# A two-stage image network on one core: fewer rows in the copies of offsets, and residuals kept in the padded image

## What is computed

```python
x = x + _L0_conv_ref(_gn(x), L0_conv_sigma)        # gaussian blur, 11 x 11
x = x + _L1_conv_ref(_gn(x), ...)                  # 3 x 3 conv -> one gate per image and channel; silu(x*scale + 0.1*x)
x = x + _L2_conv_ref(_gn(x), ...)                  # snake convolution: 9 taps, rows displaced by learned offsets, group norm, relu
x = x + _L3_conv_ref(_gn(x), ...)                  # deformable 3 x 3 convolution

def _gn(v, G=32, eps=1e-05):                       # 32 groups of one channel
    m = jnp.mean(g, axis=(2, 3, 4), keepdims=True)
    s = jnp.var(g, axis=(2, 3, 4), keepdims=True)
    return ((g - m) / jnp.sqrt(s + eps)).reshape(v.shape)
```

## Time and profile before

| what | us |
|---|---|
| median of 3 runs (3099.09 to 3121.86) | 3119.48 |
| profiled execution | 3101.79 |
| its span | 3099.4 |
| TensorE busy | 2375.4 |
| VectorE busy | 1678.2 |
| ScalarE busy | 1526.1 |
| GpSimd busy | 1000.5 |

### The profile page before, as it was taken

How to read it: one execution, slowest core, us unless ns; L and a number is a source line. 1 busy time by engine, 2 the same in 40 slices (tenths; PEclk the granted TensorE clock), 3 DMA queues, 4 the chain that set the end, 5 groups by cost and what they waited for, 6 DMA issues and landing times. The chain is left out here.

```text
span 3099.4 us, 96185 instructions
## 1 busy us (share of the span) xinstructions
PE 2375.4 (77%) x43661; PEld 1592.3 (51%) x43661; DVE 1678.2 (54%) x2736; ACT 1526.1 (49%) x1565; POOL 1000.5 (32%) x733
## 2 busy tenths in 40 slices
PE   0775991759999447698998925799992768989897
PEld 0773341537777324365655514577771434555555
DVE  5894657145555454455665461555553545555564
ACT  1222444225555434466666532455553435666665
POOL 0330001045555100444444210555541014444442
PEclk7997995879999768798999957899996777899999
DMA  1568515011110542989889651011107248798986
GB/s 50 166 190 146 87 26 217 11 39 28 30 29 24 186 172 62 187 219 223 218 222 225 152 222 32 19 37 26 30 23 281 84 96 192 191 223 205 222 220 148
DMA packets 254017, 399.94 MB, mean 129 GB/s; under 512 B 85741, under 2 KB 180513, under 8 KB 237217
## 3 DMA queue, kind: packets, MB, share of 16 engines
q1 hardware_dynamic: 244384, 360.16, 46.3%
q0 software_dynamic: 9216, 33.56, 2.6%
HBM read 295.08 MB, written 98.57 MB: 127 GB/s over the span
## 5 line engine op out<-in xcount | busy, mean ns | idle before, releaser
L1426 ACT ACTIVATE snake_samp<-snake_s 128x1024 f32<-128x1024 f32 x320 | 320.9, 1023 | 299.9 <-PE snake_s L1356 299.8
L2164 PE MATMUL dense_spread<-dense_cp,kept_spread_x 32*128 32x512 f32 x1280 | 369.1, 678 | 116.7 <-DVE dense_hat L2313 53.4
L1489 DVE TENSOR_SCALAR snake_hat<-snake_spread 128x1024 f32<-128x1024 f32 x256 | 301.5, 1219 | 205.4 <-PE snake_spread L1334 205.4
L2267 ACT ACTIVATE dense_samp<-dense_s 128x864 f32<-128x864 f32 (+1 forms) x384 | 295.9, 807 | 234.6 <-PE dense_s L2204 232.9
L2313 DVE SCALAR_TENSOR_TENSOR dense_hat<-dense_hat,dense_spread 128x1024 f32<-128x1024 f32 x256 | 300.9, 1217 | 144.1 <-ACT dense_hat L2248 86.6
L2204 PEld LDWEIGHTS dense_s<-dense_hat,dense_xt 64*64 64x64 f32 x11264 | 293.2, 139 | 158.5 <-issue 78.0
L2204 PE MATMUL dense_s<-dense_hat,dense_xt 64*64 64x108 f32 x11264 | 343.0, 265 | 31.4 <-issue 16.8
L1356 PE MATMUL snake_s<-snake_hat,snake_xt 64*64 64x128 f32 x10240 | 337.7, 274 | 19.3 <-ACT snake_samp L1426 19.1
L2248 ACT ACTIVATE dense_hat<-dense_ys,kept_y_shift 128x2048 f32<-128x2048 f32 (+1 forms) x128 | 283.7, 2216 | 122.7 <-DMA dense_ys<-offs 122.7
L1356 PEld LDWEIGHTS snake_s<-snake_hat,snake_xt 64*64 64x64 f32 x10240 | 285.1, 134 | 85.7 <-issue 42.1
L660 PE MATMUL dcnoff_acc<-xn,kept_w_off 32*32 32x512 f32 x4608 | 178.1, 626 | 153.7 <-PEq L46 153.7
(11 more groups left out here) (314 smaller groups left out, 3544.2 us busy)
## 6 DMA issues: line engine op xcount, KB each, us to landing
dense_ys<-offs SPq DMA_DIRECT2D x256, 320.0 KB, 9.2
dense_ys<-offs SPq DMA_DIRECT2D x256, 256.0 KB
dense_cp<-offs SPq DMA_DIRECT2D x256, 128.0 KB
x<-blur_x SPq DMA_DIRECT2D x16, 1024.0 KB, 5.0
pre<-snake_ob SPq DMA_DIRECT2D x32, 512.0 KB, 4.0
dense_xr<-x SPq DMA_DIRECT2D x64, 256.0 KB, 5.6
out<-dense_xr SPq DMA_DIRECT2D x64, 256.0 KB, 9.1
gateconv_low<-x SPq DMA_DIRECT2D x24, 512.0 KB, 9.4
```

The costliest lines, as they stand in the source:

```text
L1426: act.activation(samp[u % 2][:, :, i * MS:(i + 1) * MS, :, :].rearrange("p b m t h -> p b (m t h)"), sample_at(u, i)[:, :, :], ACT.Copy).t ...
L1489: ins = dve.tensor_scalar(strided(hat[u % 2][:, 0:1], GUARD + (4 * tau + 2 * half) * SW * SR, [[8, 2], [SW * SR, 2], [SR, SW], [1, 8]]), s ...
L2164: return pe.matmul(bank[:, :], k.spread_x[r, kind, :], cp[u % 2][r, tile, :], start=True, stop=True)
L2267: act.activation(samp[:, :, :, :, n0 * PW:x1].rearrange("p b t r x -> p b (t r) x"), sample_at(u, i)[:, :, 0:nn * PN].rearrange("p b (t x) ...
```

## The change

- load_y copies each image's row to 24 partitions (8 to 31 of the image's 32) in place of 32; the other 8 are cleared once.
- load_x copies seven levels x 4 images = 28 partitions in place of 32; the rest of cp is cleared once. So the whole of ys and cp is cleared at the start of dcn_dense(), ahead of the first copy.
- residual() no longer keeps the stream in DRAM. VectorE adds into the inside of xn, and xn is normalized in place. x2 is rebuilt as xn * std + (mean, kept aside) by a scalar_tensor_tensor; the Relu form loads `pre` alone, and nothing is stored.
- In dcn_dense() GpSimd's new restore(u) writes xr = xn * std + shift (shift holds the means and the bias), VectorE's finish() adds xr into mod, and mod is stored. keep_mod(u) waits for the store of unit u - 2 in place of its finish(). load_x3 goes.
- A function restore() writes x3 for the branch that isn't taken here.

```diff
-def residual(nc, k, base, inner, func, scale, bias, result, xn, g):
+def residual(nc, k, source, first, func, scale, bias, xn, g):
...
-                sp.dma_start(xg[:, u * UR:(u + 1) * UR, :], base_v[:, u * UR:(u + 1) * UR, :]).then_inc(loaded[u], 16)
+                sp.dma_start(xg[:, u * UR:(u + 1) * UR, :], source[:, u * UR:(u + 1) * UR, :]).then_inc(loaded[u], 16)
...
-            for u in range(NU):
-                pool.wait_ge(sum_ready, u + 1)
-                pool.dma_start(result_v[:, u * UR:(u + 1) * UR, :], xg[:, u * UR:(u + 1) * UR, :]).then_inc(stored, 16)
-            pool.wait_ge(stored, 16 * NU)
...
-                dve.tensor_tensor(v, v, act_out[u % SLOTS][:, :, :], ALU.add).then_inc(sum_ready, 1)
+                r0 = PAD + u * UR
+                v = xn[:, r0:r0 + UR, inside]
+                if first:
+                    dve.wait_ge(loaded[u], 16)
+                    ins = dve.tensor_tensor(v, xg[:, u * UR:(u + 1) * UR, :], act_out[u % 3][:, :, :], ALU.add)
+                else:
+                    ins = dve.scalar_tensor_tensor(v, v, k.std[:, :], act_out[u % 3][:, :, :], ALU.mult, ALU.add)
...
+            v = xn[:, PAD + ACT_ROWS:PAD + H, inside]
+            dve.tensor_scalar(v, v, coef[:, 0:1], coef[:, 1:2], ALU.mult, ALU.add)
+            dve.tensor_copy(k.std[:, :], std[:, :])
...
-                    sp.dma_start(cp[u % 2][32 * i:32 * i + 32, 0:2, :],
-                                 bass.AP(tensor=at.tensor, offset=at.offset, ap=[[0, 8], [4 * OFF_CH * BX, GI], [1, 2 * BX]])
+                    sp.dma_start(cp[u % 2][32 * i:32 * i + 28, 0:2, :],
+                                 bass.AP(tensor=at.tensor, offset=at.offset, ap=[[0, 7], [4 * OFF_CH * BX, GI], [1, 2 * BX]])
...
-                    sp.dma_start(ys[part][32 * b:32 * b + 32, :, :].rearrange("p t x -> p (t x)"),
-                                 bass.AP(tensor=at.tensor, offset=at.offset, ap=[[0, 32], [1, len(PARTS[part]) * BX]])
+                    sp.dma_start(ys[part][32 * b + 8:32 * b + 32, :, :].rearrange("p t x -> p (t x)"),
+                                 bass.AP(tensor=at.tensor, offset=at.offset, ap=[[0, 24], [1, len(PARTS[part]) * BX]])
...
-                sp.dma_start(out_v[:, 4 * u:4 * u + 4, :], xr[:, :, :]).then_inc(stored, 16)
+                sp.dma_start(out_v[:, 4 * u:4 * u + 4, :], mod[u % 2][:, :, :]).then_inc(stored[u % 2], 16)
...
-                if u >= 1:
-                    sp.wait_ge(stored, 16 * u)
-                    load_x3(u)
...
-                ins = pool.memset(cp[i][:, 2, :], 0.0)
+                pool.memset(ys[i][:, :, :], 0.0)
+                ins = pool.memset(cp[i][:, :, :], 0.0)
...
+            def restore(u):
+
+                if u >= 1:
+                    pool.wait_ge(out_done, u)
+                r0 = PAD + 4 * u
+                pool.tensor_scalar(xr[:, :, :], xn[:, r0:r0 + 4, PAD:PAD + W], k.std[:, :], k.shift[:, :], ALU.mult, ALU.add
+                                   ).then_inc(x3_ready, 1)
...
                 if u >= 2:
-                    act.wait_ge(out_done, u - 1)
+                    act.wait_ge(stored[u % 2], u // 2 * 16)
                 act.activation(mod[u % 2][:, :, :].rearrange("p r x -> p (r x)"), p_hat[0][:, 1, :], ACT.Copy).then_inc(mod_kept, 1)
...
-                dve.scalar_tensor_tensor(xr[:, :, :], mod[u % 2][:, :, :], k.vec('L3_conv_bias'), xr[:, :, :], ALU.add, ALU.add).then_inc(out_done, 1)
+                dve.tensor_tensor(mod[u % 2][:, :, :], mod[u % 2][:, :, :], xr[:, :, :], ALU.add).then_inc(out_done, 1)
```

More of the change, by code:

```diff
@@ L1008, in residual @@
         xg = s.sb("x", [P, H, W])
-        SLOTS = 2 if inner is None else 8
-        act_out = [s.sb(f"act{i}", [P, UR, W]) for i in range(SLOTS)]
+        act_out = [s.sb(f"act{i}", [P, UR, W]) for i in range(3)]
         st = s.sb("stats", [P, 2 * NU, 6])
@@ L1015, in residual @@
         loaded = [s.sem(f"loaded{i}") for i in range(NU)]
-        inner_loaded = [s.sem(f"inner_loaded{i}") for i in range(SLOTS)]
         chain = s.sem("vector_chain")
+        ring_clear = s.sem("ring_clear")
         act_ready = s.sem("act_ready")
         sum_ready = s.sem("sum_ready")
-        stored = s.sem("stored")
         var_ready = s.sem("var_ready")
@@ L1087, in _, with restore @@
             dve.wait_ge(coef_ready, 1)
-            dve.tensor_scalar(xn[:, PAD + ACT_ROWS:PAD + H, PAD:PAD + W], xg[:, ACT_ROWS:H, :], coef[:, 0:1], coef[:, 1:2], ALU.mult, ALU.add)
+            v = xn[:, PAD + ACT_ROWS:PAD + H, inside]
+            dve.tensor_scalar(v, v, coef[:, 0:1], coef[:, 1:2], ALU.mult, ALU.add)
+            dve.tensor_copy(k.std[:, :], std[:, :])
+            if first:
+                dve.tensor_copy(k.mean[:, :], mv[:, 0:1])
+            else:
+                link(dve.tensor_tensor(k.mean[:, :], k.mean[:, :], mv[:, 0:1], ALU.add))
+                dve.tensor_tensor(k.shift[:, :], k.mean[:, :], k.vec('L3_conv_bias'), ALU.add)
+def restore(nc, k, xn, x3, g):
+    x3_v = x3.rearrange("(g b) c h w -> g (b c) h w", g=NG)[g]
+    NU = 8
+    UR = H // NU
+    with ExitStack() as ctx:
+        s = Space(nc, ctx, f"restore{g}")
+        xg = s.sb("x", [P, H, W])
+        ready = s.sem("ready")
+        stored = s.sem("stored")
+        block = ctx.enter_context(nc.Block())
+        @block.scalar
+        def _(act):
+            for u in range(NU):
+                act.activation(xg[:, u * UR:(u + 1) * UR, :], xn[:, PAD + u * UR:PAD + (u + 1) * UR, PAD:PAD + W], ACT.Identity,
+                               bias=k.mean[:, :], scale=k.std[:, :]).then_inc(ready, 1)
+        @block.sync
+        def _(sp):
+            for u in range(NU):
+                sp.wait_ge(ready, u + 1)
+                sp.dma_start(x3_v[:, u * UR:(u + 1) * UR, :], xg[:, u * UR:(u + 1) * UR, :]).then_inc(stored, 16)
+            sp.wait_ge(stored, 16 * NU)
 def snake_offsets(nc, k, xn, steps, g):
@@ L2005, in _, with dcn_dense @@
                     dve.tensor_copy(keep[:, r0:r0 + R, GI * MOD + b], p_t[v % 2][:, :, MOD]).then_inc(keep_ready, 1)
-def dcn_dense(nc, k, xn, offs, x3, out, g):
-    x3_v, out_v = (t.rearrange("(g b) c h w -> g (b c) h w", g=NG)[g] for t in (x3, out))
+def dcn_dense(nc, k, xn, offs, out, g):
+    out_v = out.rearrange("(g b) c h w -> g (b c) h w", g=NG)[g]
     NB4 = H // 4
@@ L2056, in dcn_dense @@
         scale_done = s.sem("scale_done")
-        x3_in = s.sem("x3_in")
+        x3_ready = s.sem("x3_ready")
         out_done = s.sem("out_done")
-        stored = s.sem("stored")
+        stored = [s.sem(f"stored{i}") for i in range(2)]
         block = ctx.enter_context(nc.Block())
@@ L2099, in _ @@
             load_x(1)
-            load_x3(0)
             for part in range(2):
@@ L2115, in _ @@
                     load_x(u + 3)
-                if u >= 1:
-                    sp.wait_ge(stored, 16 * u)
-                    load_x3(u)
             store(NB4 - 1)
-            sp.wait_ge(stored, 16 * NB4)
+            for slot in range(2):
+                sp.wait_ge(stored[slot], 16 * (NB4 // 2))
         @block.gpsimd
@@ L2158, in _ @@
                 keep_even(u)
+                restore(u)
         @block.tensor
@@ L2379, in build @@
             with nc.If(dense > 0):
-                dcn_dense(nc, k, xn, offs[g], x3, out, g)
+                dcn_dense(nc, k, xn, offs[g], out, g)
             with nc.Else():
+                restore(nc, k, xn, x3, g)
                 offsets_by_row(nc, k, offs[g], by_row, g)
```

48 lines of the change are left out of this document (20 added, 28 removed).

## The result

| | us |
|---|---|
| before, median of 4 runs (3099.09 to 3121.86) | 3110.19 |
| changed, median of 4 runs (3320.61 to 3327.93) | 3325.12 |
| ratio, 95% interval | 1.0689 (1.0637 to 1.0741) |

The change makes the kernel 6.9% slower. The forecast was 3170 with a range to 3245. The profiled execution has a span of 3322.8 us, 223.4 more than before.

What follows compares the result with a forecast made beforehand. The dense stage was taken as DMA-bound at 16.23 us a unit, rising to 17.6. Profiled 3101.8 + 77 (56 units) + 14 (memsets) - 42 (residual) + 1 = 3152; +50 on the median 3119.5 gave 3170 us, range 3005 to 3245.

Steps and rivals of the forecast that it cites:

- Part 2: Dense stage: not loading x3 takes 0.7 us off the unit's queue; GpSimd's operation rebuilding it was taken to cost 0.
- Part 3: Dense stage: keep_mod waits for the store's landing behind the y copies; loop 17.0 us a unit, TensorE standing 2.8.
- clock term: Dense stage: after a stand TensorE runs at its lower clock; 0.6 us a unit taken, range 0 to 1.9.
- rival D: Dense stage far slower: the clock falls in every unit, or y meets its upper bound, 19.5; 3275 us, chance 0.10.
- Part 1: Dense stage: y copies of 24 rows on 12 engines take as long as 32 on 16; smaller copies worth 0.
- Part 4: Start of dcn_dense(): GpSimd's larger memsets take 6.8 us more, twice, with nothing hiding it; +14 us.
- Part 5: residual(): the Relu form falls to VectorE's pace, 21 us saved, twice; -42 us; the Silu form 0.
- Rival A: Dense stage faster: the landing is covered, so a unit costs its DMA alone, 14.9 us; 3018 us, chance 0.13.

Runs made afterwards that it cites:

- e2: Kernel before plus one GpSimd wait for finish() of the unit before, placed after keep_even(u), without the restore operation; 3265.4 us (one run).
- e6: Changed kernel with VectorE's clip as a scalar_tensor_tensor whose upper bound lies in PSUM, GpSimd's order kept; 3171.3 us (one run).
- e10: Changed kernel with VectorE's clip(u+2) moved ahead of finish(u-1); 3174.2 us, 1.0213 to the kernel before.
- e1: Changed kernel with GpSimd's restore(u) moved between the two halves of stage(u+2); 3169.2 us, 1.0198 to the kernel before.
- e17: e14 with y copies of 32 rows and x copies of eight levels again; 3100.3 us, 0.9974 to the kernel before.
- e14: e1 with the output put together in xn's rows, so keep_mod waits for finish(u-2) and no landing; 2992.3 us, 0.9628 to the kernel before.

## Why the prediction was wrong

- **Part 2 failed**: "It waits for finish() of the unit before and stands ahead of stage() ... were that cover gone, a unit would lose up to 1 us. I take 0." The step asked when stage()'s result is needed, and that was no problem. It didn't ask what runs on other engines at the time to which stage() moves. The wait moved a run of 8.8 us of GpSimd's work so that its end lies on VectorE's clip, and a unit takes 20.5 us where 17.6 was forecast. e2 shows that the wait alone does it, e6 and e10 that it is the clip. Price: 3325 against the 3169 of e1, some 156 us.
- **Part 3 was right as a mechanism in part, and hidden in the result.** Once the collision is gone keep_mod waits for the landing, in 55 of e1's 64 units, 2.3 us each by the mean, and TensorE stands behind it in 19 of them, not in each. The mean unit is 17.84 us where 17.6 was forecast, made of units of 15.4 to 21.3, and in 14 of the 26 units from 1316 to 1780 TensorE stands for VectorE's product behind the slowed clip instead (21.9 us, and 21.6 for keep_mod). e1 is at 3169, the forecast's 3170, but with one cause taken out that the forecast didn't have; the agreement is partly luck. In the changed kernel itself its sign ("keep_mod waiting some 3 us") is absent.
- **The clock term** was right in kind and too small for the changed kernel: 3.1 us in each unit (1.8 + 1.3), where 0.6 was taken and 1.9 was the bound. A stand of some 3.65 us brought the lower clock in every unit, as rival D had it, though D had it from the landing. That a late TensorE takes away the idle time was an argument without a row.
- **Part 1**: the 12 engines are confirmed (152 small packets, three quarters of the share), the worth of 0 isn't. It was 0.8 us a unit in the kernel before and 1.9 between e17 and e14, x copies included. Shown is that the y parts pass 6% sooner and that the engines' share in the dense stage falls (0.72 in e14, 0.90 in e17 over the same stretch, 0.90 before from 1300 to 1748 us); how the time is saved beyond that, whether x copies and stores use the engines that y leaves free, wasn't tested. Two of its readings were a little off: by share its rows give 13.5 and 13.9 GB/s for an engine, not both 13.9, and TensorE's 14.6 us at 0.96 are 14.0, not 14.2 (e14: 14.1).
- **Part 4**: the four memsets take 6.6 us (1217.28 to 1223.89) in place of 1.0; 11 us for both groups, 14 forecast. Right.
- **Part 5**: the Relu stage ends its statistics 45.4 us after its start (66.7 before), 21.3 saved, 21 forecast; the sum takes 1269 ns where 1217 was taken. Right.
- **Rival A** was the right idea for a kernel that wasn't built: with the landing off the path (e14) the time is 2992, and 3018 was forecast for it. Its unit of 14.9 us also equals the mean of e14's two groups (15.3 and 14.5), but that is luck: A had DMA set the unit, and in e14's second group the DMA share is 0.72 and TensorE is full.

The account of the 223.4 us: 28 units in each group +240, clearing +11, Relu stages -42; the +14 that remain lie in the other four units of each group or the other stages, and weren't followed.
